# An attention and feed-forward block: the score ring runs on over chunks, and the first chunk's order of work is changed

## What is computed

```python
C_q = x @ Wq_d + bq_d                  # 12 latents per token
C_kv = x @ Wkv_d + bkv_d               # 4 latents per token
q = (C_q @ W_qk + b_qk).reshape(b, s, 32, 4)
scores = einsum('bqhd,bkd->bhqk', q, C_kv) / sqrt(4)
attn = softmax(scores, axis=-1)
V = (C_kv @ Wv_u + bv_u).reshape(b, s, 32, 32)
out = einsum('bhqk,bkhd->bqhd', attn, V).reshape(b, s, 1024)
attention = out @ Wo + bo

x = x + attention(layernorm(x))
h = layernorm(x)
x = x + h @ W.T + bias + sum over n of (2 * lora_weights[n]) * (h @ lora_A[n].T) @ lora_B[n].T
```

## Time and profile before

| | us |
|---|---|
| median of 3 runs | 2167.85 (2167.52 to 2172.3) |
| the profiled execution | 2171.91 |
| its span | 2170.1 |
| TensorE busy | 1954.2 (90%) |
| ScalarE busy | 2005.0 (92%) |
| VectorE busy | 511.2 (24%) |
| GpSimd busy | 180.3 (8%) |
| mean share of 16 DMA engines | 10.6% |

### The profile page before, as it was taken

One profiled execution on the slowest core, in us unless ns is written; L12 is line 12 of the kernel. 1 busy time (PEld: TensorE's weight loads), 2 busy tenths in 40 slices (PEclk: granted clock), 3 DMA queues, 4 the chain that ended last, 5 costly groups with the idle time before them and its releaser, 6 DMA issues. The chain is left out here.

```text
span 2170.1 us, 35966 instructions
## 1 busy us (share of the span) xinstructions
PE 1954.2 (90%) x15023; PEld 717.3 (33%) x15023; DVE 511.2 (24%) x1292; ACT 2005.0 (92%) x2193; POOL 180.3 (8%) x100
## 2 busy tenths in 40 slices
PE   5748888799999999899999999899989999899989
PEld 3412222233333333233333333233333333233337
DVE  8732133212102110212102120212102120212125
ACT  6948999999999999999999999999999999999960
POOL 1210001000100001100100001100100000100111
PEclk9978999999999999999999999999999999999999
DMA  7432201000010000100010000100010000100010
GB/s 239 175 81 87 83 15 35 5 4 25 25 44 6 13 26 25 34 14 14 25 44 6 14 24 25 34 15 13 25 44 6 19 19 25 35 16 14 24 39 39
DMA packets 49116, 78.99 MB, mean 36 GB/s; under 512 B 17790, under 2 KB 33206, under 8 KB 48954
## 3 DMA queue, kind: packets, MB, share of 16 engines
q1 hardware_dynamic: 48954, 76.69, 10.6%
HBM read 52.02 MB, written 24.64 MB: 35 GB/s over the span
## 5 line engine op out<-in xcount | busy, mean ns | idle before, releaser
L554 ACT ACTIVATE probs<-ps 128x1024 f32<-128x1024 f32 x2048 | 1911.5, 1029 | 64.7 <-PE ps L765 37.9
L776 PE MATMUL ps<-probs,c_wide 128*32 128x512 f32 x8192 | 990.6, 601 | 0.0
L765 PE MATMUL ps<-q_in,key_t 30*128 30x512 bf16 x4096 | 405.2, 385 | 146.4 <-ACT probs L554 137.1
L821 PE MATMUL ps<-w_eff,xn_t 128*128 128x512 f32 x1344 | 387.0, 416 | 0.0
L765 PEld LDWEIGHTS ps<-q_in,key_t 30*128 30x128 bf16 x4096 | 103.8, 91 | 766.5 <-ACT probs L554 712.0
L776 PEld LDWEIGHTS ps<-probs,c_wide 128*32 128x32 f32 x8192 | 213.3, 109 | 427.3 <-issue 241.3
L1230 DVE TENSOR_TENSOR y<-ps,y 128x512 f32<-128x512 f32 x64 | 44.3, 692 | 965.2 <-PE ps L821 954.9
L821 PEld LDWEIGHTS ps<-w_eff,xn_t 128*128 128x128 f32 x1344 | 230.4, 188 | 98.5 <-issue 63.5
L460 POOL TENSOR_TENSOR y<-y,ffn_bias 128x1024 f32<-128x1024 f32 x32 | 76.2, 2381 | 1169.4 <-DVE xn L987 1169.4
L456 POOL TENSOR_TENSOR y<-y,attn_bias 128x1024 f32<-128x1024 f32 x32 | 76.2, 2383 | 704.8 <-DMA y<-in_L_attn_x_dram 704.6
L1009 DVE CAST xn_t<-ps 128x512 fp32r<-128x512 f32 x64 | 44.2, 691 | 158.9 <-PE ps L806 158.9
(11 more groups left out here) (130 smaller groups left out, 598.6 us busy)
## 6 DMA issues: line engine op xcount, KB each, us to landing
y<-in_L_attn_x_dram SPq DMA_DIRECT2D x48, 512.0 KB, 4.2
out_dram<-y SPq DMA_DIRECT2D x32, 512.0 KB, 2.7
area<-in_L_attn_x_dram SPq DMA_DIRECT2D x16, 512.0 KB, 4.5
q_in<-q_parts SPq DMA_DIRECT2D x256, 30.0 KB, 1.7
q_parts<-q_parts_sb SPq DMA_DIRECT2D x48, 128.0 KB, 2.1
y<-in_L_attn_Wo_dram SPq DMA_DIRECT2D x1, 2048.0 KB, 8.5
xn<-in_L_attn_Wo_dram SPq DMA_DIRECT2D x1, 2048.0 KB, 13.5
y<-in_L_ffn_W_dram SPq DMA_DIRECT2D x1, 2048.0 KB, 8.0
```

Of the source, the lines that this page charges most:

```text
L554: nc.scalar.activation(probs[:, (c * STEPS + step) % PROBS, bass.ts(pair, 2 * N)], ps[:, 2 * (i % SCORE_SLOTS):2 * (i % SCORE_SLOTS) + 2, ...
L765: last = nc.tensor.matmul(ps[:, at, :], key_t[TILE * h:TILE * h + KEYS, bass.ts(b * KT + kt, P)], q_in[TILE * h:TILE * h + KEYS, g % 2, :] ...
L776: last = nc.tensor.matmul(ps[32 * h:32 * h + 32, SUMS, :], c_wide[:, b * KT + kt, at:at + 32], probs[:, (c * STEPS + step) % PROBS, bass.t ...
L821: last = nc.tensor.matmul(ps[:, SHARED, :], xn_t[:, t % 2, a, kb, :], w_eff[:, b, kb, bass.ts(half, N)], start=(kb + i == 0), stop=(kb == ...
```

## The change

- The contraction has 27 rows for 30. Blocks with key part 1 and 2 no longer have a shift row (`SHIFT_BLOCKS` = 3, `BLOCK_AT`), and only three shift rows are stored per chunk. The copies to `spread` are made block by block, 24 for 4.
- The query parts (`q_parts`) have their own room. ScalarE no longer waits for query stores at step 1; at its first exponential it waits until the last latents are split.
- SyncE stores the first chunk's shifts, loads the first group's queries, and then stores the other shifts of the first sequence.
- VectorE's `weigh(1)` stands inside the last `split_latents`, no longer behind it.
- The slots of the score ring are counted over all chunks, and the wait at a chunk's first step is that of all others.
- TensorE's wait for the next group's queries stands behind the scores of step 15 of a group for ahead of step 0.
- The preparation: values at step 17 for 7, LoRA at 19 and 21 for 9 and 13, Wo from 23, biases at 39 and 41, weight blocks from 43 (five before the outputs' turn at 67, eleven from 69 on).

```diff
-    KEYS = BLOCKS * W5
+    SHIFT_BLOCKS = KEY_PART.index(1)
+    BLOCK_AT = [W5 * i - max(i - SHIFT_BLOCKS, 0) for i in range(BLOCKS + 1)]
+    KEYS = BLOCK_AT[BLOCKS]
...
-        q_parts = nc.alloc_sbuf_tensor_at("q_parts_sb", [P, 2, PARTS, N], BF16, offset=probs_at + 4 * 4 * N)
+        q_parts = sb("q_parts_sb", [P, 2, PARTS, N], BF16)
...
-            def store_shifts(b):
-
-                sp.wait_ge(shift_split, b + 1)
-                for j in range(CB):
-                    for i in range(BLOCKS):
+            def store_shifts(b, first, last):
+
+                for j in range(first, last):
+                    for i in range(SHIFT_BLOCKS):
...
-            store_shifts(0)
+            sp.wait_ge(shift_split, 1)
+            store_shifts(0, 0, 1)
 
             sp.wait_ge(q_stored[0], Q_STORES * (CHUNKS // 2))
-            sp.wait_ge(first_shift, BLOCKS * 16)
+            sp.wait_ge(first_shift, SHIFT_BLOCKS * 16)
             load_q(0, 0, 0, q_loaded[0])
+            store_shifts(0, 1, CB)
             for c in (CHUNKS - 2, CHUNKS - 1):
                 store_q(c, c % 2)
-            store_shifts(1)
+            sp.wait_ge(shift_split, 2)
+            store_shifts(1, 0, CB)
...
-                        i = 2 * step + pair
-                        act.wait_ge(s_ready, c * 2 * STEPS + i + 1)
-                        if pair == 0 and first and step == 1:
-
-                            for slot in range(2):
-                                act.wait_ge(q_stored[slot], Q_STORES * (1 + CHUNKS // 2))
+                        i = 2 * (c * STEPS + step) + pair
+                        if i == 0:
+                            act.wait_ge(lat_split, START + CHUNKS)
+                        act.wait_ge(s_ready, i + 1)
...
-                if step:
-                    pe.wait_ge(exp_done, 2 * (c * STEPS + step) - 1)
-                elif not first:
-                    pe.wait_ge(exp_done, 2 * c * STEPS)
+                i = 2 * (c * STEPS + step)
+                if step or not first:
+                    pe.wait_ge(exp_done, i - 1)
                 for h in range(4):
-                    at = 2 * ((2 * step + h // 2) % SCORE_SLOTS) + h % 2
+                    at = 2 * ((i + h // 2) % SCORE_SLOTS) + h % 2
...
-
-                    pe.wait_ge(q_loaded[g % 2], (c * (G4 // 2) + g // 2 + 1) * Q_LOADS)
                     for kt in range(KT):
                         step = g * KT + kt
                         scores(c, b, step, first)
+                        if kt == KT - 1 and c * G4 + g + 1 < CHUNKS * G4:
+                            pe.wait_ge(q_loaded[(g + 1) % 2], ((c * G4 + g + 1) // 2 + 1) * Q_LOADS)
...
             for h in range(4):
-                ch.put(nc.vector.tensor_copy(spread[:, TILE * h:TILE * h + KEYS].rearrange("p (i d) -> p i d", d=W5)[:, :, 0:L],
-                                             fold[:, 0:L].unsqueeze(1).to_broadcast([P, KEYS // W5, L])))
+                for i in range(BLOCKS):
+                    at = TILE * h + BLOCK_AT[i]
+                    ch.put(nc.vector.tensor_copy(spread[:, at:at + L], fold[:, 0:L]))
...
-            split_latents(CB + 3, 1, lambda: largest(1))
-            weigh(1)
+            split_latents(CB + 3, 1, lambda: (largest(1), weigh(1)))
```

More of the change, by code:

```diff
@@ L276, in build_block @@
         PREP_ALL = PREP_W + 4 * KB
+        VALUES_AT = 17
+        WO_AT = VALUES_AT + 6
+        BIAS_AT = WO_AT + 16
+        W_AT = BIAS_AT + 4
+        TURN_0_AT = 4 * KT + 3
+        W_BEFORE = (4 * KT - W_AT) // 4
         @block.sync
@@ L314, in store_q @@
                 for i in range(BLOCKS):
-                    sp.dma_start(qd[:, i * W5:i * W5 + L, bass.ds(c * N, N)], q_parts[:, slot, QUERY_PART[i], :]).then_inc(q_stored[slot], 16)
+                    sp.dma_start(qd[:, BLOCK_AT[i]:BLOCK_AT[i] + L, bass.ds(c * N, N)], q_parts[:, slot, QUERY_PART[i], :]).then_inc(q_stored[slot], 16)
             for half in range(2):
@@ L358, in _ @@
                     sp.wait_ge(m_split, c + 1)
-                    for i in range(BLOCKS):
+                    for i in range(SHIFT_BLOCKS):
                         sp.dma_start(qd[:, i * W5 + L, bass.ds(c * N, N)], shift_parts[0:H, QUERY_PART[i], :]).then_inc(m_stored, 16)
-                    sp.wait_ge(m_stored, BLOCKS * 16)
-                    sp.sem_inc(m_stored, -BLOCKS * 16)
+                    sp.wait_ge(m_stored, SHIFT_BLOCKS * 16)
+                    sp.sem_inc(m_stored, -SHIFT_BLOCKS * 16)
                 sp.wait_ge(q_loaded[0], Q_LOADS)
@@ L737, in prepare @@
             def prepare(g, kt):
[L738 removed]
+                step = g * KT + kt
+                if step == VALUES_AT:
                     turn_values()
[L740 to L753 removed]
+                if step in (VALUES_AT + 2, VALUES_AT + 4):
+                    turn_lora(PREP_LORA + (step - VALUES_AT) // 4)
+                if WO_AT <= step < WO_AT + 16 and step % 2:
+                    i = (step - WO_AT) // 2
+                    times_wo(PREP_VO + i // 2, lv if i < 4 else bv_wide, i % 2)
+                if step in (BIAS_AT, BIAS_AT + 2):
+                    sum_bias(PREP_BIAS + (step - BIAS_AT) // 2)
+                for k in range(2 * KB):
+                    at = W_AT + 4 * k if k < W_BEFORE else TURN_0_AT + 2 + 4 * (k - W_BEFORE)
+                    if step == at:
+                        turn_w(k)
+                    if step == at + 2:
+                        lora_update(k)
             def scores(c, b, step, first):
                 g, kt = divmod(step, KT)
[L759 to L762 removed]
+                i = 2 * (c * STEPS + step)
+                if step or not first:
+                    pe.wait_ge(exp_done, i - 1)
                 for h in range(4):
[L764 removed]
+                    at = 2 * ((i + h // 2) % SCORE_SLOTS) + h % 2
                     last = nc.tensor.matmul(ps[:, at, :], key_t[TILE * h:TILE * h + KEYS, bass.ts(b * KT + kt, P)],
@@ L887, in attention @@
                             turn_o(c - 1, 1)
-                        if first and kt == 3 and g == 4:
-                            pe.wait_ge(prep_ok, PREP_W + 8)
+                        if first and step == TURN_0_AT:
+                            pe.wait_ge(prep_ok, PREP_W + 2 * W_BEFORE)
                             turn_o(c, 0)
@@ L1084, in _ @@
             for h in range(4):
-                for i in range(KEYS // W5):
-                    ch.put(nc.vector.tensor_copy(bias_row[:, TILE * h + W5 * i:TILE * h + W5 * i + L], bkv_row))
-                ch.put(nc.vector.memset(bias_row[:, TILE * h:TILE * h + W5 * KEY_PART.index(1)]
+                for i in range(BLOCKS):
+                    at = TILE * h + BLOCK_AT[i]
+                    ch.put(nc.vector.tensor_copy(bias_row[:, at:at + L], bkv_row))
+                ch.put(nc.vector.memset(bias_row[:, TILE * h:TILE * h + W5 * SHIFT_BLOCKS]
                                         .rearrange("p (i d) -> p i d", d=W5)[:, :, L:W5], 1.0))
@@ L1231, in add_dense @@
                                         ).then_inc(ffn_moved, 1)
-            for k in range(4):
+            for k in range(W_BEFORE):
                 move_w(k)
@@ L1236, in _ @@
             norm_o(0, 0)
-            for k in range(4, 2 * KB):
+            for k in range(W_BEFORE, 2 * KB):
                 move_w(k)
```

26 lines of the change are left out of this document (6 added, 20 removed).

## The result

The changed kernel takes 2145.37 us (median of 5 runs, 2144.14 to 2146.86), the kernel before 2167.85 (2167.51 to 2172.3): a ratio of 0.9894, interval 0.9882 to 0.9905, or 22.5 us less. Forecast were 2143.5 us and 24.3 us. The profiled execution of the changed kernel took 2144.14 us, its span is 2142.2.

What follows compares the result with a forecast made beforehand. It took the time as a prologue, 2048 ScalarE exponentials in a row, and a tail. First chunk 14.3, ring 8.65 and moved wait 1.3 us sum to 24.3 us off 2167.85, giving 2143.5 us; range 2136 to 2152 (8 in 10).

Steps and rivals of the forecast that it cites:

- Late load of the second group's queries, five us given back: First chunk, step 16: queries issued behind the weights land at 167.9, holding exponential 32 and giving back 5 us.
- the first rival: Second group's queries land 4.1 us after first issue, so exponential 32 isn't held: 6.6 us more gain, 2137 us; chance 0.12.
- First exponential at 11.3 us: First chunk's start: first exponential at 132.3 for 138.36, taking 1.6 us from `tight` to the first scores.
- `tight` 1.2 us earlier: VectorE in the prologue: moving `weigh(1)` ahead of the last latents' split has the branch-deciding value written at 130.0.
- SyncE's queue: First chunk's start: with fewer shift stores the preparation's weights go out at 147.0 for 157.99, 11.0 us earlier, perhaps 12.
- LoRA block at step 19: First chunk: VectorE's 32 small copies take 6.7 us for two steps of 3.7, stopping ScalarE before exponential 40.
- Half-clock holes: First chunk: TensorE at half clock after the second group's query wait, charged as one hole of 1.7 us.
- Ring: Chunk boundaries: 1.0 us gained at each of 7, plus 1.65 us for a clock hole at the first, 8.65 us in all.
- Moved wait: Head group starts: 0.09 us each, 14 in chunks 1 to 7 for 1.3 us, plus 0.4 us in the first chunk.
- 2 (boundaries stay): Chunk boundaries keep their holes because another wait replaces the ring's; without the 8.65 us it is 2152; chance 0.13.
- 3: First chunk gives all its gain back through late load and LoRA wait at half clock, 2158 us; chance 0.06.
- 4: TensorE stays at half clock in the first chunk after step 16, making it slower, up to 2199 us; chance 0.03.

Runs made afterwards that it cites:

- e14: The changed kernel run again unchanged (third time), beside the kernel before on another chip: 2145.08 us, ratio 0.9891.
- e9: The changed kernel with TensorE's slower branch written once, in one loop over all chunks, so the jumped-over code is about half as long: 2144.27 us, ratio 0.9889.
- e0: The changed kernel run again unchanged, as base for the first batch: 2145.43 us, ratio 0.9896.
- e2: The changed kernel with the score ring started over at slot 0 in each chunk: 2151.54 us, ratio 0.9923.
- e4: The changed kernel with TensorE's wait for the next group's queries back ahead of the group's first scores: 2147.22 us, ratio 0.9902.
- e5: The changed kernel with 30 rows and all six shift stores per chunk kept: 2159.36 us, ratio 0.9960.
- e12: The changed kernel with the second head group's queries loaded ahead of the preparation's weights: 2138.98 us, ratio 0.9868.
- e8: The changed kernel with the values turned at step 15 for 17, LoRA blocks still at 19 and 21: 2141.86 us, ratio 0.9885.
- e1: The kernel before with only the score ring counted over all chunks: 2162.07 us, ratio 0.9974.
- e6: The changed kernel with query parts back in the probabilities' room and ScalarE waiting for query stores at its third exponential: 2144.88 us, ratio 0.9893.
- e7: The changed kernel with the preparation at its old steps (values at 7, LoRA at 9 and 13): 2146.24 us, ratio 0.9901.

## Why the prediction was right, step by step

- **Late load of the second group's queries, five us given back** (the forecast's main mechanism): right in e14 and e9 (5.64 and 5.29 us of wait ended by the DMA), 1.88 us long in e0, 3.62 in e2, 3.19 in e4, and absent in the changed kernel's first profile. By the prediction's own sign ("I am wrong if exponential 32 is not held by a DMA") that profile contradicts it. Two things that the forecast didn't have used up the time there: the longer branch (3.4 us) and a second hole at half clock (1.58). That exponential 32 still stands at 47.2 us, for 47.5 forecast, is luck; the mechanism is shown by e14, e5 and e12, not by the profile of the result. Its price was right: the first rival put 6.6 us on a load that isn't late, and e12 gained 6.1.
- **First exponential at 11.3 us** behind the first shift store: 10.3 with a short branch, 13.9 with a long one. The step that failed is TensorE's way from `tight` to the first scores, 1.6 us "a little above SyncE's remainder": it is 1.4 (126.75 to 128.18 in e14) or 4.98. The bounds, nothing to 6.5, held both; that both occur in one program I had not seen.
- **`tight` 1.2 us earlier**: it is 8.2 us behind the first shift store (126.78 - 118.60) for 10.2, 2.0 earlier; undersized, without effect.
- **SyncE's queue**: 12.1 us for 11.0, but not for the reason allowed for. Of the 1.1 us the four loads of 27 rows give 1.35 (1.37 us for 2.72) and the nine stores 0.5; the twelve query stores take 1.2 back (8.80 for 7.64); the gaps between the pieces give the other 0.4.
- **LoRA block at step 19**: VectorE's copies hold it in every profile of the changed kernel, the stop before exponential 40 is 3.03 and 1.50 us for 3.4 and 1.03. In e8, with two steps more, both go.
- **Half-clock holes**: I charged one of 1.7 us; the first profile has two, 2.07 and 1.58.
- **Ring**: 6.4 us in the trace and 6.1 by the medians (5.2 in e1) for 7.0, and 1.65 charged for a clock hole that e2 doesn't have. That hole was read from a profile 4.1 us over the median and then taken off the median.
- **Copies to `spread`**: the text sets 0.08 us each without a row; the earlier trace rows has 0.42 / 4 = 0.105. The 24 took 1.80 us for 0.42 and cost nothing, the first tile's statistics start at 5.47 for 5.57.
- **Moved wait**: 2.2 us (1.8 by the medians) for 1.3 and the 0.4 in the first chunk.
- **Sum**: by the medians the ring gives 6.1, the wait 1.8, and so the first chunk 22.5 - 7.9 = 14.6, where the forecast had 14.3 - 0.4 = 13.9. The ring term was 2.5 us too large, the first chunk 0.7 too small and the wait 0.1; that is the difference of 1.8 us. Inside the first chunk two errors cancel: in e14 the load ends TensorE's wait 1.6 us earlier than forecast, and from exponential 32 to 42 it takes 16.6 us for 15.4.
- **Rivals**: 2 (boundaries stay) fell with the one row of 2006 exponentials, 3 with exponential 42 on time, 4 with the clock, at 1.00 from 178.9 to 2076 us. 1 had its sign (no stop at exponential 32) in one profile, but not its reason: where TensorE waited for them, the queries came not 4 us but 13 us after their issue (150.50 to 163.82 in e14, 152.67 to 166.17 in e0).

Not tried: `weigh` at its old place, and the order of the first sequence's stores around the first load, by themselves.

## What to carry to other kernels

Ask of each earlier start which wait stands next and whether it moves too; here the first exponential came 3.6 us sooner or later and the time stayed within its scatter, since a load further down one queue set exponential 32. A queue shared by urgent small loads and large weights is worth an order of its own: four loads of 27 KB moved ahead of 4 MB gave 5 to 6 us, and stores of rows that multiply zeros, left out, gave 14. Two waits close behind each other hide one another, so undoing one part alone (e6, e7) can read as nothing, and a part that gains 7 us at the first exponential (e5) can be gone twenty steps later.

## What the hardware showed that I had not expected

One branch instruction of TensorE takes 0.46 us in some executions and 3.5 to 4.1 in others of the same program. In two batches it was short and in one long for every kernel (e9, with other code to jump over, had 0.36). The prologue's end moved too: the first shift store was issued at 121.04 us in the profile of before and between 116.79 and 119.96 in all thirteen after it. e1, whose prologue is that of the kernel before, has 119.96 and the twelve others at most 119.30, so a small part may be the change's; that isn't shown. By the medians there is no room for 2.4 us: ring, wait and first chunk make 6.4 + 2.2 + 14.3 = 22.9 us in the traces (exponential 42 at 62.5 in e14), for 22.5 measured.
